# Cross attention with heads of 32: maxima from bf16 pieces in three products, VectorE makes the pieces and drains half of keys and values

## The reference, cut to what matters

```
H, D, C1, C2, S, M, B, W = (16, 32, 128, 64, 256, 64, 2, 4)
xn = _ln(x, lnx_g, lnx_b)
yn = _ln(y, lny_g, lny_b)
q = jnp.einsum('bsc,hcd->bhsd', xn, wq)
k = jnp.einsum('btc,hcd->bhtd', yn, wk)
v = jnp.einsum('btc,hcd->bhtd', yn, wv)
a = jax.nn.softmax(jnp.einsum('bhsd,bhtd->bhst', q, k) * D ** (-0.5), axis=-1)
o = jnp.einsum('bhst,bhtd->bhsd', a, v)
x_out = x + o @ li1_w + li1_b
```

## Time and profile before

| | |
|---|---|
| median of three executions | 4032.26 us (4030.01 to 4044.68) |
| the profiled execution's own time | 4038.64 us |
| its span | 4036.9 us |
| busy: PE, VectorE (DVE), ScalarE (ACT), GpSimd (POOL) | 3242.3, 2389.7, 1805.8, 1094.5 us |
| the maxima's matmuls (L2178) | 2048 records, 1519.0 to 2614.3 us |
| the maxima's reduces (L2282) | 352, 483.1 us busy, 476.7 us idle before them for PE |
| the exponentials (L2257) | 384, 372.2 us busy, 358.0 us idle before them |
| GpSimd's additions (L2330) | 128, 579.1 us busy |

### The profile page before, as it was taken

How to read it: one execution, slowest core, us unless ns; L and a number is a source line. 1 busy time by engine, 2 the same in 40 slices (tenths; PEclk the granted TensorE clock), 3 DMA queues, 4 the chain that set the end, 5 groups by cost and what they waited for, 6 DMA issues and landing times. The chain is left out here.

```text
span 4036.9 us, 81036 instructions
## 1 busy us (share of the span) xinstructions
PE 3242.3 (80%) x33476; PEld 1634.2 (40%) x33476; DVE 2389.7 (59%) x3851; ACT 1805.8 (45%) x2194; POOL 1094.5 (27%) x767
## 2 busy tenths in 40 slices
PE   7985999999588827999999999977876799999821
PEld 5661333332266513444444444444542233333311
DVE  4554788878456454555555555433435688688676
ACT  2321677676333223444444444432211477677611
POOL 1002112110233253655565656631001111111000
PEclk9995999999799867999999999988877799899965
DMA  0003111110000030000000000001202211111000
GB/s 26 2 12 69 44 32 33 34 38 11 17 22 2 1 76 6 10 10 2 10 10 10 2 10 2 2 1 33 59 17 50 50 33 39 34 41 27 2 6 11
DMA packets 69858, 89.94 MB, mean 22 GB/s; under 512 B 37582, under 2 KB 50427, under 8 KB 69499
## 3 DMA queue, kind: packets, MB, share of 16 engines
q1 hardware_dynamic: 65642, 78.37, 8.6%
q10 hardware_dynamic: 3856, 6.47, 0.9%
HBM read 34.17 MB, written 4.33 MB: 10 GB/s over the span
## 5 line engine op out<-in xcount | busy, mean ns | idle before, releaser
L1970 DVE TENSOR_REDUCE mx<-ps 128x2 f32<-128x802 f32 (+1 forms) x1372 | 1028.2, 778 | 292.5 <-PE ps L1836 267.5
L1904 ACT ACTIVATE probs<-ps 128x1024 f32<-128x1024 f32 (+1 forms) x832 | 832.9, 1024 | 257.1 <-PE ps L1822 248.3
L2282 DVE TENSOR_REDUCE mx<-ps 128x3 f32<-128x1203 f32 (+1 forms) x352 | 483.1, 1373 | 476.7 <-PE ps L2178 476.7
L2330 POOL TENSOR_TENSOR sums<-sums,probs 128x2048 f32<-128x2048 f32 x128 | 579.1, 4524 | 143.7 <-ACT probs L2257 129.0
L1836 PE MATMUL ps<-kt,qs 48*128 48x401 bf16 x2048 | 472.4, 355 | 115.2 <-DVE mx L1970 79.0
L2257 ACT ACTIVATE probs<-ps 128x1024 f32<-128x1024 f32 x384 | 372.2, 1021 | 358.0 <-PE ps L2156 357.9
L1854 PE MATMUL ps<-probs,v_cur 128*9 128x256 f32 x6656 | 530.0, 391 | 0.4 <-ACT probs L1904 0.4
L2178 PE MATMUL ps<-kt,qt 32*128 32x401 f32 x2048 | 339.8, 556 | 46.4 <-DVE mx L2282 40.8
L1822 PE MATMUL ps<-qs,kt 50*128 50x256 bf16 (+1 forms) x3328 | 346.3, 281 | 1.8 <-ACT probs L1904 1.4
L2011 POOL CAST max_pieces<-negm 128x8 bf16<-128x8 f32 x64 | 12.1, 189 | 1122.2 <-DVE negm L1975 1122.2
L1836 PEld LDWEIGHTS ps<-kt,qs 48*128 48x128 bf16 x2048 | 134.6, 95 | 331.8 <-DVE mx L1970 255.6
(11 more groups left out here) (402 smaller groups left out, 4268.0 us busy)
## 6 DMA issues: line engine op xcount, KB each, us to landing
kt<-k SPq DMA_DIRECT2D x776, 50.0 KB
ctx_s<-in_ctx_t SPq DMA_DIRECT2D x16, 400.2 KB, 4.6
ctx_s<-ctx_norm_t SPq DMA_DIRECT2D x16, 400.2 KB, 5.5
qs<-q ACTq DMA_DIRECT2D x24, 192.0 KB
ctx_norm_t<-ctx_norm_t SPq DMA_DIRECT2D x8, 400.2 KB
ctx_a<-in_ctx_t SPq DMA_DIRECT2D x8, 400.2 KB
ctx_b<-in_ctx_t SPq DMA_DIRECT2D x8, 400.2 KB
ctx_tok<-in_ctx SPq DMA_DIRECT2D x8, 384.0 KB
```

The costliest lines, as they stand in the source:

```text
L1904: act.activation(pr[0:m, u % 3, :], pair[0:m].rearrange("p a n -> p (a n)"), ACT.Exp, scale=scale).then_inc(s_free, 1)
L1970: dve.tensor_reduce(mx[:, n % 2, i0:i0 + count], src, AX_X, ALU.max).then_inc(freed(step), 1)
L2282: dve.tensor_reduce(mx[:, n % 2, 3 * i0:3 * i0 + count], rbanks[:, 0:count, 0:CH], AX_X, ALU.max).then_inc(ring_free, 1)
L2330: pool.tensor_tensor(o, o, p, ALU.add).then_inc(added, 1)
```

## The change

The maxima's product of fp32 queries and keys becomes three bf16 products that accumulate in the same bank: high x high, low x high, high x low, where high is the value rounded to bf16 and low the bf16 rounding of the rest. The pieces are made on VectorE, for the keys in each `kproj` step and for the queries in each `qproj` step. VectorE also copies out two of the four banks of each `kproj` and `vproj`, ScalarE the other two; a second semaphore, `s_shared`, counts VectorE's share, and TensorE waits for both. `kt` has three buffers in place of four. The list `period` is written anew: the key step stands behind `max 7` (it stood behind `max 9`), weigh 0 and 1 come together behind scores 3, weigh 6 goes into the next group, `sums` and `take` later.

More of the change, by code:

```diff
@@ L2046, in wide_plan @@
                 plan.append((kind, g, *part))
-    slot, ring = {}, {}
+    slot, ring, shared = {}, {}, {}
     for step in plan:
+        if step[0] in ("kproj", "vproj"):
+            shared[step] = len(shared)
         if step[0] in ("scores", "kproj", "vproj", "qproj"):
@@ L2052, in wide_plan @@
             ring[step] = len(ring)
-    return plan, slot, ring
+    return plan, slot, ring, shared
 def wide_cross(nc, k, scale, ctx_t, xt, wq, wk, wv, w1, b1, x, xo):
-    plan, slot, ring = wide_plan()
+    plan, slot, ring, shared = wide_plan()
     with ExitStack() as ctx:
@@ L2062, in wide_cross @@
         ctx_s = sb("ctx_s", [P, 2, LC])
-        kt = sb("kt", [P, 4, LC])
+        kt = sb("kt", [P, 3, LC])
+        kh, kl = sb("k_high", [P, 2, LC], BF16), sb("k_low", [P, 2, LC], BF16)
+        qh, ql = sb("q_high", [P, 2, GT, S], BF16), sb("q_low", [P, 2, GT, S], BF16)
         v = sb("v_cur", [P, 2, KT, P])
@@ L2089, in wait_drained, with wait_slot @@
             eng.wait_ge(s_free, slot[step] + 1)
+            if step in shared:
+                eng.wait_ge(s_shared, shared[step] + 1)
+        def wait_slot(pe, step):
+            wait(pe, s_free, slot[step])
+            wait(pe, s_shared, sum(slot[s] < slot[step] for s in shared))
         def wait_ring(eng, step):
@@ L2124, in _ @@
                     b = step[1]
-                    wait(pe, s_free, slot[step])
+                    wait_slot(pe, step)
                     for a in range(GT):
@@ L2155, in _ @@
                         for j in range(4):
-                            ins = pe.matmul(sbanks[0:m, j, S * i:S * i + S], kt[rows(j), n % 4, P * t:P * t + m],
+                            ins = pe.matmul(sbanks[0:m, j, S * i:S * i + S], kt[rows(j), n % 3, P * t:P * t + m],
                                             qt[rows(j), b % 2, a, :], start=False, stop=(i == last))
@@ L2265, in _ @@
                     n = step[1]
[L2266 to L2267 removed]
+                    if n >= 3:
+                        wait_filled(act, ("scores", n - 3, NW - 1))
                     wait_filled(act, step)
[L2269 to L2271 removed]
+                    act.activation(kt[:, n % 3, 0:2 * CH].rearrange("p (a n) -> p a n", n=CH), sbanks[:, 0:2, 0:CH],
+                                   ACT.Copy).then_inc(s_free, 1)
         @block.vector
@@ L2289, in _ @@
                                           negate=True).then_inc(placed, 1)
+                elif kind == "vproj":
+                    n = step[1]
+                    wait(dve, pv_done, NW * (n - 1))
+                    wait_filled(dve, step)
+                    dve.tensor_copy(v[:, n % 2, 0:KT - 1, :].rearrange("p (a b) c -> p b a c", b=4)[:, 2:4],
+                                    sbanks[:, 2:4, 0:3 * P].rearrange("p b (a c) -> p b a c", c=P)).then_inc(s_shared, 1)
+                elif kind == "kproj":
+                    n = step[1]
+                    if n >= 3:
+                        wait_filled(dve, ("scores", n - 3, NW - 1))
+                    wait_filled(dve, step)
+                    (lo, mid), (_, hi) = CHUNKS[2:4]
+                    dve.tensor_copy(kt[:, n % 3, lo:mid], sbanks[:, 2, 0:mid - lo])
[7 more added lines that the diff above has]
+                elif kind == "qproj":
+                    b = step[1]
+                    if b >= 2:
+                        wait_ring(dve, ("max", GT * (b - 2) + GT - 1, 10))
+                    wait_drained(dve, step)
+                    dve.tensor_copy(qh[:, b % 2, :, :], qt[:, b % 2, :, :]).then_inc(q_cut, 1)
+                    dve.wait_ge(q_cut, 2 * b + 1)
+                    dve.tensor_tensor(ql[:, b % 2, :, :], qt[:, b % 2, :, :], qh[:, b % 2, :, :],
+                                      ALU.subtract).then_inc(q_cut, 1)
                 elif kind == "neg":
```

7 lines of the change are left out of this document (4 added, 3 removed).

## The result

| | median | runs | ratio to before, 95% interval |
|---|---|---|---|
| before, same chip | 4038.47 us | 4030.01 to 4045.15 (4) | 1 |
| after | 4116.78 us | 4098.60 to 4126.09 (4) | 1.019 (1.0143 to 1.0237) |

The change makes the kernel 1.9% slower, some 78 us. The forecast was 4235, a loss of some 200 us, in a range of 4035 to 4290; the measured time is close to rival 1's 4119. The profiled run of after took 4126.09, its span 4124.3, against 4036.9 before.

A forecast was written before the change was run, and what follows sets the result against it. Three chains of nearly one length (maxima ring, scores, PE) bound the kernel, the ring after the change. Profiled 4038.6 + 176 (hold) + 25 (clock) = 4240; the median lies 6 lower: 4235 us, range 4035 to 4290.

The forecast's parts named there:

- rival 1: VectorE's cast waits for addition 3, the subtraction does not wait: 36.7 us a group, +74, 4119 us; chance 0.25.
- PE's step of maxima: Three bf16 products per maxima step take PE 0.63 us instead of 0.88, 2.7 us a group saved.
- Rival 4: Maxima's bf16 products don't overlap their weights, 0.80 a step: +33 to +37 on any case; chance 0.2 within each.
- VectorE's added work: Drains and pieces add 4.92 us a group, queries' pieces 0.5; VectorE goes from 17.7 to 23.1.
- The sum with nothing held: New order with added work at its own durations: 34.44 us a group against 34.29, +7 us over 31 groups.
- The clock, +25: PE's idle time brings 1.2 GHz back each group: bounds 0 and 1.6 us a group, half taken, 25 us.
- the 7 us hole of every group: PE waits 7 us at max 9, as max 8 is reduced at 11.64 instead of 4.21.
- The mechanism of the hold: VectorE's key cast waits out GpSimd's addition 3 (3.07 + 1.00), then the subtraction waits out addition 4 (near 6.3, not 1.83).
- the size of the hold: VectorE's pieces meeting GpSimd's additions: mean 40.0 us a group, +5.7 a group, +176 us over the stage.
- the keys are drained 10.8 us behind those exponentials: From window 1's exponentials to the key drain's end; the cast then asks with 3.1 us of addition 3 left.
- Rivals 2 and 3: 2: pieces run beside additions, +7, 4040, chance 0.13; 3: nothing held, PE step 0.50, -22 us, 4010, chance 0.12.
- The pattern of periods: Key-drain periods by group: plain 40.05, the output's 36.94, the queries' 42.99, mean 40.0 us.

The follow-up runs named there:

- warm_small_adds: Changed kernel with five extra rounds of overwritten maxima products in step 5 and GpSimd's additions cut to 8 columns: 4039.47 us, 1.0024 to before.
- warm: Changed kernel with five extra rounds of overwritten maxima products in step 5, in TensorE's idle time: 4172.22 us, 1.0361 to before.
- small_adds: Changed kernel with GpSimd's four additions a group cut from 2048 columns to 8: 4064.36 us, 1.0099 to before.
- order_only: Kernel before with only the new list `period` (fp32 maxima, all drains on ScalarE, no pieces): 4091.33 us, 1.0158 to before.
- split_only: Changed kernel with fp32 maxima and no pieces, keeping the new list and split drains: 4069.30 us, 1.0080 to before.
- searched_order: bf16 maxima, pieces on GpSimd, all drains on ScalarE, and another list found by writing out the queues: 3994.72 us, 0.9899 to before.

## Why the prediction was right and where it was wrong

- **PE's step of maxima: right.** 0.63 was forecast, 0.61 measured. In order of time, PE's products and what follows, and VectorE's reduce:

```profile
2080.74 0.34 PE L2192 MATMUL ps<-k_high,q_high 32*128 32x401 bf16 x3
2080.74 0.10 PEld L2192 LDWEIGHTS ps<-k_high,q_low 32*128 32x128 bf16 x3
2080.91 0.34 PE L2192 MATMUL ps<-k_high,q_low 32*128 32x401 bf16 x3
...
2081.08 0.34 PE L2192 MATMUL ps<-k_low,q_high 32*128 32x401 bf16 x3
...
2081.35 1.07 PE L2213 MATMUL ps<-probs,v_cur 128*32 128x256 f32 x16
2081.54 1.41 DVE L2295 TENSOR_REDUCE mx<-ps 128x3 f32<-128x1203 f32 x1 [0.89 <-PE ps L2192]
```

  The weights of the second product load beside the first, in the same row groups. The Trainium skill (TensorE: Matmul & The Clock Gate, Part 3, The mechanism) says in one place that loads overlap only where the row group differs; here the measurement decides against it. It fits the other half that the prediction drew on, the background buffer. Rival 4 is out.
- **VectorE's added work: right** to 0.03 us for each instruction. The sum with nothing held was +7 us (the written-out means, 34.44 and 34.29, give 5 over 31 groups). warm_small_adds, the nearest to it, came out as +10 (0 to 19 by its interval), with a part of the clock's fall still in it (0.96).
- **The clock, +25: its mechanism right where a group is held, its place wrong for the rest.** It was put behind the 7 us hole of every group. It does fall there in the five groups that are held twice (0.50 from 2124 to 2126), but in 24 it falls ahead of the key step, at the idle times of 0.95 and 1.64, where the forecast had nothing. Its size is not measured: the 30 us of the extra rounds are those of another stretch, so that they lie near 25 is luck.
- **The mechanism of the hold: right**, both halves of it. Where a cast meets the third addition 10.5 us behind the first, it takes 4.22 for a forecast of 4.07, and the subtraction 6.00 for 6.35; the hold of a subtraction behind an addition, which no row had shown, is shown. The Trainium skill (SBUF — State Buffer, Who interferes with whom) has it so: a VectorE instruction with two SBUF inputs blocks fully against a GpSimd one that reads SBUF.
- **The step that failed is the size of the hold: 176 us forecast, 36 measured** (13 to 59, or 62 by the profiled periods). The term rests on one interval, "the keys are drained 10.8 us behind those exponentials", and takes it for every group. It was walked at full clock, while the clock was then added to the sum as a cost of its own. The two are not independent. In 24 groups of 30 a slow stretch like that of 1919 to 1925 lies inside that interval and puts the cast at 12.1 to 14.3 us behind the first addition, where it finds at most 1.7 us left of the third, which is over at 13.8. Only six groups start at 10.3 to 10.5, and five of them are held twice. The run warm shows it by putting the interval back to 10.5 in most groups: against warm_small_adds the hold then costs 135 us, clock behind the holes included, where the forecast's two terms make 201.
- **The rivals.** Rival 1 named 4119 and the time is 4116.78, but not for its reasons. Its picture, the cast waits and the subtraction does not, is that of most groups, but with a wait of 0 to 1.6 us for its 3.1 and a period of 37.83 for its 36.7, and the subtraction is held wherever it meets the fourth addition. That number is right by accident. Rivals 2 and 3 are refuted for after; as small_adds shows, even without a meeting order and clock lose 1.0%, some 40 us, where the forecast had 7 for the order and all of the clock's 25 behind the hold.
- **The pattern of periods** (40, 40, 37, 43) did not come: 46.2, 46.7, 40.8, 40.9 and 46.6 behind the five double holds, 34.4 to 37.8 elsewhere. In warm it nearly did: 41.5, 41.2, 37.7 and 36.6, over and over, with a single hold in the group of 37.7 as forecast; only the group forecast at 43 is not held twice, since the clock falls ahead of its key step. The stage's clock, 0.90, came as forecast, but mostly from the slow stretch ahead of the key step.

What stays open: why two idle times of 0.90 and 1.64 lower the clock in one group and not in the next, and how much of order_only's 1.6% is its clock (0.97) and how much the longer chain; in split_only, at 0.99, 0.8% remains. No run keeps the clock at 1.00 in the change's list, so what the clock costs there in all is not measured.

## What to carry to other kernels

Two losses on one path are to be walked together: one that shifts when an instruction asks for a shared resource can hide or expose the other, and the sum of the two is then wrong in either direction. Before work is moved to an engine with room, look at what stands behind it in that engine's queue and who waits for that: here 2.8 us ahead of a reduce on VectorE, the less busy of the two, made the kernel 3.3% slower than 4.7 us between additions on GpSimd. Price a cheaper product by the order it runs in: the same bf16 maxima were worth 1.0% in one list and nothing in another.

## What was not expected of the hardware

- Filling TensorE's idle time with products that are thrown away changes the time both ways: -0.7% with nothing to hold (1.0099 to 1.0024), +1.7% with the additions there.
- The granted clock fell to 0.50 after idle times of 0.95 and 1.64 us with little work between them (1915 to 1919: PE busy 2.02 of 4 us), and stayed there for some 6 us. It fell behind the first of the two alone in nine groups, and in others stayed at 1.00 behind both.
- A held VectorE instruction ends as if it had begun when the addition ended, to 0.2 us: the subtraction of 6.00 from 2116.15, less its own 1.83, begins at 2120.3, and the fourth addition ends at 2120.47. GpSimd's own cast (1.52) and subtraction (3.0 to 3.3) were not held in any of 32 groups of searched_order, while VectorE read PSUM beside them.
